# Last layer of a four-layer kernel: where the head outputs' copy, normalising and addition stand in the order of work

## The reference

```python
    q, k, v = (split_heads(einsum('bsd,kd->bsk', x, w)) for w in (q_proj_weight, k_proj_weight, v_proj_weight))
    scores = einsum('bhtc,bhkc->bhtk', q, k) * head_size ** -0.5
    scores = where(causal, scores, -inf)
    attn = softmax(scores, axis=-1)
    out = einsum('bhtk,bhkc->bhtc', attn, v)
    return einsum('bsv,dv->bsd', merged(out), o_proj_weight)
```

## Time and profile before

| what | us |
|---|---|
| median of 3 runs (lowest, highest) | 3794.77 (3785.83, 3804.28) |
| span of the profiled execution | 3867.5 |
| stretch in which units attend, in the profile | 2880 to 3867.5 |

### The profile page before, as it was taken

How to read it: one execution, slowest core, us unless ns; L and a number is a source line. 1 busy time by engine, 2 the same in 40 slices (tenths; PEclk the granted TensorE clock), 3 DMA queues, 4 the chain that set the end, 5 groups by cost and what they waited for, 6 DMA issues and landing times.

```text
span 3867.5 us, 47778 instructions
## 1 busy us (share of the span) xinstructions
PE 3519.2 (91%) x16468; PEld 2089.1 (54%) x16468; DVE 2473.4 (64%) x6381; ACT 1730.0 (45%) x3237; POOL 1164.8 (30%) x1190
## 2 busy tenths in 40 slices
PE   8899999968898988989878999998899999999998
PEld 7677777734555545545546667676543333433332
DVE  4444443455788988889865443443568788678774
ACT  2234443322234423343344544443346666666667
POOL 0322222151355555555542322223211111011111
PEclk7799999988899999999989999999889899999999
DMA  3244445321466666666750000000101011111100
GB/s 109 73 165 168 177 180 180 128 66 71 136 204 193 216 211 194 197 204 197 212 187 3 0 1 1 1 1 9 38 20 31 20 23 34 31 34 27 32 18 23
DMA packets 107154, 368.87 MB, mean 95 GB/s; under 512 B 27248, under 2 KB 41088, under 8 KB 96928
## 3 DMA queue, kind: packets, MB, share of 16 engines
q0 software_dynamic: 57664, 302.82, 24.3%
q1 hardware_dynamic: 48160, 60.90, 5.6%
q10 hardware_dynamic: 1088, 2.10, 0.2%
HBM read 322.59 MB, written 17.69 MB: 88 GB/s over the span
## 4 chain that ended last, share of the span: by engine, by line
PE 66%; DVE 21%; ACT 6%; issue 4%; another core or an unknown queue 2%; POOL 1%; DMA 0%; POOLq 0%; DVEq 0%; SPq 0%; ACTq 0%
PE ps L184 51%; PE ps L2636 6%; DVE pm L2784 4%; PE ps L1507 2%; DVE mi L1642 2%; DVE gathB L1719 2%; DVE ps L2787 2%; DVE hacc L1682 2%; ACT P L2917 1%; PE ps L2126 1%; DVE mx L1638 1%; PE ps L556 1%; PE ps L581 1%; PE ps L546 1%
## 5 line engine op out<-in xcount | busy, mean ns | idle before, releaser
L2917 ACT ACTIVATE P<-ps 128x512 f32<-128x512 f32 (+3 forms) x1280 | 587.3, 548 | 214.1 <-PE ps L184 212.0
L2784 DVE TENSOR_REDUCE pm<-ps 128x1 f32<-128x512 f32 x768 | 484.6, 684 | 113.3 <-PE ps L184 113.0
L1860 POOL DMA_INDIRECT gathB<-in_tab,idx x256 | 282.9, 1105 | 357.6 <-PE ps L1507 287.4
L184 PE MATMUL ps<-QS,KS 49*128 49x512 f32 (+3 forms) x1280 | 333.8, 422 | 16.2 <-DVE pm L2784 12.6
L1860 POOL DMA_INDIRECT gathA<-in_tab,idx x256 | 268.7, 1049 | 203.2 <-DVE mx L1638 125.5
L184 PE MATMUL ps<-KS,QS 48*128 48x512 f32 (+3 forms) x1280 | 309.8, 430 | 16.0 <-DVE pm L2787 5.9
L2974 POOL TENSOR_SCALAR_AFFINE_SELECT P<-P 128x256 f32<-128x256 f32 x256 | 103.8, 409 | 709.9 <-ACT P L2917 709.0
L2636 PE MATMUL ps<-P,Va 128*32 128x512 f32 (+3 forms) x2560 | 309.7, 557 | 5.8 <-POOL P L2974 2.9
L184 PEld LDWEIGHTS ps<-QS,KS 49*128 49x128 f32 x1280 | 158.2, 190 | 225.0 <-DVE pm L2784 81.8
L184 PEld LDWEIGHTS ps<-KS,QS 48*128 48x128 f32 x1280 | 145.5, 191 | 212.8 <-DVE pm L2784 66.2
L2787 DVE CUSTOM_DVE_ANT_0 ps<-ps,past 128x128 f32<-128x128 f32 (+3 forms) x512 | 240.1, 515 | 26.6 <-PE ps L184 24.6
(11 more groups left out here) (390 smaller groups left out, 7002.8 us busy)
## 6 DMA issues: line engine op xcount, KB each, us to landing
ys_sorted<-moe SPq DMA_DIRECT2D x71, 128.0 KB
KS<-hi SPq DMA_DIRECT2D x256, 32.0 KB, 1.9
QS<-hi SPq DMA_DIRECT2D x256, 32.0 KB, 1.9
gathA<-in_tab,idx POOLq DMA_INDIRECT x256
gathB<-in_tab,idx POOLq DMA_INDIRECT x256
KS<-lo SPq DMA_DIRECT2D x128, 32.0 KB, 1.9
QS<-lo SPq DMA_DIRECT2D x128, 32.0 KB, 2.0
out<-xT SPq DMA_DIRECT2D x8, 512.0 KB, 3.2
```

The costliest lines, as they stand in the source:

```text
L184: m = pe.matmul(out, w, x, start=start and i == 0, stop=stop and i == len(pairs) - 1, skip_group_check=True)
L1860: pool.indirect_dma_start(out=(GA, GB)[half][:, h, :], out_offset=None, in_=d[f"tab{half}"], in_offset=bass.IndirectOffsetOnAxis(ap=idx[t ...
L2784: v = dve.tensor_reduce(m, p, AX.X, ALU.max)
L2917: act.activation(P_[:, hh, off:BW], psx.tile("s2", j, n, kt, pr, hh)[:, off:BW], ACT.Exp).then_inc(*psx.emptied(MN.act, "s2", j, n, kt, pr ...
```

## The change

The copy of `o` moves from the end of a unit into the generator `finish`: it is now issued in the first step of the next unit, behind that unit's two exponentials of (kt 0, pr 0). Two empty yields follow it, so Ln stands in step 3 and Exp in step 4. On PE the sum moves from step 1 to step 2, and the two attn matmuls from steps 6 and 7 to 7 and 8; DVE's two additions move with them. The two waits ahead of the copy move with it. POOL's program is as it was.

```diff
@@ pe_main
                 def finish(n):
+                    yield
                     p = psx.fill("sum", j, n)
                     pe.wait_ge(*MN.act.has("o", j, n))
@@ dve_main
-                    yield from nothing(5)
+                    yield from nothing(6)
@@ act_main
                 def finish(n):
                     act.wait_ge(*MN.pool.has("on", *((j, n - 1) if n else (j - 1, 3))))
+                    act.wait_ge(*MN.pe.has("pv", j, n, 4 * n + 3))
+                    act.activation(osb[:, :], po.tile("o", j, n)[:, :], ACT.Copy).then_inc(*po.emptied(MN.act, "o", j, n))
+                    yield from nothing(2)
                     act.wait_ge(*MN.pe.has("sum", j, n))
                     act.activation(inv[:, :], psx.tile("sum", j, n), ACT.Ln).then_inc(*psx.emptied(MN.act, "sum", j, n))
                     yield
@@ act_main, end of a unit
-                act.wait_ge(*MN.pool.has("on", *((j, n - 1) if n else (j - 1, 3))))
-                act.wait_ge(*MN.pe.has("pv", j, n, 4 * n + 3))
                 tail.drain()
-                act.activation(osb[:, :], po.tile("o", j, n)[:, :], ACT.Copy).then_inc(*po.emptied(MN.act, "o", j, n))
                 tail.gen = finish(n)
```

## The result

| | before | after |
|---|---|---|
| median of 4 runs each, us | 3794.47 | 3835.14 |
| lowest, highest | 3785.83, 3804.28 | 3820.19, 3852.51 |
| span of the profiled execution | 3867.5 | 3849.6 |
| attending, first pv to last pv, in the profile | 982.6 | 1019.8 |
| of it at half clock | 73.6 | 124.8 |

The ratio is 1.0104, 95% interval 1.0069 to 1.0138: some 40 us slower. The forecast was 13 us slower, 3780 to 3832, so the direction was right and the size wrong, outside the range by 3 us. The two spans must not be compared: the profiled execution of before reached its first pv at 2873.3 us, that of after at 2817.2, for code that is the same in both. The attending stretch, which the change touches, is 37.2 us longer, which is nearly the whole difference of the medians, 40.7.

A forecast was written before the change was run, and what follows sets the result against it. PE and DVE in turn, through seven shared banks, were taken to set the end. Terms 10.0 + 1.6 + 1.6 - 0.5 = 12.7 us, or 0.33%, gave 3807 us on the median; range 3780 to 3832.

The forecast's parts named there:

- The sum: The forecast's total over all kinds of unit entered and the last unit: 12.7 us slower.
- n = 0, POOL's stall: Seven entered units: POOL's divide waits for later Exp and delays kt 1's masks; 10.0 us slower, bounds 0 and 23.
- n = 2: Eight units limited by DVE: s2 of (1, 1) waits for one more reduction; 1.6 us slower, bounds 0 and 0.68 each.
- nearer to 0, since what DVE needs is already made: Choice within the n = 2 bounds of 0 and 0.68 us: 0.2 us of loss for each unit.
- n = 1 and n = 3: Sixteen units, mostly with a projection: 0.1 us of loss each, 1.6 us; bounds 0.45 gain and 0.4 loss each.
- these cancel nearly: For n = 1 and n = 3: earlier projection's 0.45 us gain against 0.4 us loss from later pv of kt 2.
- Rival 1: At unit starts, PE's wait for the copy was really lost and is given back: 23 us faster, 3772 us; chance 0.12.
- Rival 3: No difference: waits move but the periods of PE and DVE stay; 3795 us; chance 0.20.
- Rival 2: Ln and Exp delay ACT everywhere, 12.6 us more in 14 units with a projection: 25 us slower, 3820 us; chance 0.23.
- The Trainium skill's rule on repeated gaps: Repeated gaps can mean PSUM is too small; sum's bank held longer, unpriced; 0.6 us per start would make 19 us.

The follow-up runs named there:

- e11: The changed kernel run again unaltered on another chip; ratio 1.0109 to the kernel before.
- e1: The changed kernel, with POOL's multiplication in n = 0 units moved behind the masks of kt 1 instead of kt 0; ratio 1.0082.
- e2: The changed kernel with one empty yield instead of two on ACT, so Ln in step 2 and Exp in step 3; ratio 1.0031.
- e6: The kernel before with only the sum moved to step 2, and Ln and Exp behind it in steps 2 and 3; ratio 1.0087.
- e12: The changed kernel with s2 tiles made three times over, in n = 0 for kt 1 to 3, in n = 2 for (kt 0, pr 1); ratio 1.0086.
- e7: The kernel before, copy and sum in place, with Ln and Exp in steps 3 and 4, attn products and additions in 7 and 8; ratio 1.0225.
- e10: The kernel before with attn products and additions one step later, and n = 0 s2 tiles of kt 1 to 3 made three times over; ratio 0.9952.
- e8: The kernel before with only the two attn products and DVE's additions one step later; ratio 1.0010.

## Why the prediction was wrong

**The sum had no term for the clock.** It priced every wait at full clock. With 0.35 us for each us, the 51.2 us more of half clock are 18 us of the 37, and 19 are left for the waits against 13 forecast. The text weighed nothing on what PE's standing still does to the clock, though the clock records of the trace before already showed 1.2 GHz in parts of (1, 0), (1, 3), (6, 0) and (7, 0), among others. That step failed by omission. Where it falls can be read in the trace: in (4, 2), from 3383.00 to 3386.26, PE ran 8 matmuls in 3.26 us, held up by DVE, and the stretch behind it ran at half clock. The kernel before had the sum, a full 128-row product, in the same place, and kept its clock:

```profile
3383.00:3386.26 3.26, 2.75 (x8) 0.95 (x6) 3.23 (x10) 2.56 (x5) 0.00 (x0) 0.91 0.52 175
3386.26:3392.50 6.24, 6.24 (x20) 2.24 (x22) 2.55 (x5) 3.06 (x6) 0.22 (x1) 0.50 0.03 11
```

```profile
3417.60:3420.90 3.30, 2.80 (x11) 1.07 (x10) 3.27 (x9) 2.92 (x6) 0.00 (x0) 1.00 0.40 130
```

The first two lines are after, the third is before. PE's busy share hardly differs, 2.75 of 3.26 us and 2.80 of 3.30, so these rows show where the clock fell and not why.

The Trainium skill bears on this (TensorE: Matmul & The Clock Gate, Why this matters for your kernels): it warns of throughput dropping when PE stands idle for long between bursts of matmuls. Only the direction agrees. The gap that it names is longer than any here: in (2, 0) the clock fell behind 1.18 us of standstill, in (4, 2) behind 0.16 us. And a place does not meet the half clock every time, as e11 shows.

**n = 0, POOL's stall: right.** Taking 0.35 us per us of half clock off both kernels, the seven units are 22.0 - 0.35 x (68.9 - 34.8) = 10.1 us longer; forecast 10.0. That it is so near is in part luck: 12 of the 22 us are taken off for the clock at a price that is itself a fit. (5, 0) at full clock is 1.0 us longer, forecast 0.8. In (2, 0) the pv of kt 1 came 1.5 us late, forecast 0.83, but half clock had begun 3 us into the unit, with the later sum. e1 and e2 take the stall away from either side. The bounds of 0 and 23 us held.

**n = 2: too small.** 12.2 - 0.35 x (23.9 - 2.9) = 4.9 us, forecast 1.6. I took the cost near 0 because DVE had work; e6 shows 0.57 us in (2, 2) at full clock, near the other end, 0.68. The changed kernel itself has 0.35 in (2, 2), and 0.77 in (5, 2) as e11 has it at full clock, which is past the bound. The step "nearer to 0, since what DVE needs is already made" failed.

**n = 1 and n = 3: too small.** 3.0 - 0.35 x (9.9 - 6.6) + 0.35 x (20.3 - 13.0) = 4.4 us, with the last unit, against 1.1 forecast. At full clock (2, 3) takes 48.59 us (in e12, whose filler leaves n = 3 alone) where it took 48.05 before, and (2, 1) 24.63 against 24.15: both past the bound of 0.4. (4, 1) gains, 23.68 against 23.83. That "these cancel nearly" was a sum of two guesses about banks.

**The rivals.** Rival 1 fell: PE's loads waited 7 us less for the copy and nothing came of it. Rival 3 fell. Rival 2 gave 3820 us and named Ln and Exp, and e2 (one step sooner, most of the loss back) and e7 point to their lateness; e6, with Ln and Exp where e2 has them and 1.0087, does not fit that alone. Its mechanism, ACT full behind them, is not what happened: ACT's wait for PE's scores grew. What the waits show is the bank that Ln empties and the masks behind the multiplication.

**The Trainium skill's rule on repeated gaps** (Perfetto Trace Analysis, Optimization Strategy) was quoted with the right resource: in e7 the sum's bank alone makes PE stand still 45.7 us.

Open: why a given place meets half clock in one execution and not in another, as (5, 0) did in two runs of one program; and how the 19 us at full clock in the changed kernel divide between the sum's place and Ln's, whose single moves (e6, e7) do not add up to it; and why e6's ratio is three times what its profile shows.

## What to carry to other kernels

When a result is kept in a ring of buffers that others share, don't move the operation that empties it away from the one that fills it: filling it at once and emptying it two steps later cost 2.3% (e7). Moving both by one step held the bank no longer, and still cost 0.9% (e6), so it is the lesser harm and no remedy. Read unit lengths only beside the clock column, and put into every forecast a term for what a new standstill of TensorE does to its clock, here an estimate of 0.35 us for each us at half clock. Before moving work from a place where its engine waits to one where it is queued, look at who stands behind it in program order, on the other engines too.

## What the hardware showed that was not expected

Work that does nothing can pay: with 192 added matmuls and a late attn product the kernel ran 0.5% faster than before (e10), where the late attn product alone had 1.0010 (e8). Half-clock time fell from 85.2 us to 29.5, and at 0.35 us each that is 19 us, the 0.5%. And the same program's unit (5, 0) took 14.40 us in one execution and 19.72 in another, at mean clocks of 1.00 and 0.57.
